# A two-layer graph network: edge product in the second sweep, node stage inside the first

## The chip, the cores and the metric

The kernel runs on one core of one Trainium2 chip. The time is the device time of one execution in microseconds (us). Before the change three runs gave 4691.19 us as their median (4682.67 to 4695.08).

## What is computed

12,500 nodes with 128 numbers each, and 200,000 edges whose targets `dst` are sorted and lie densest at low node numbers (target = 12500·u², u uniform). Two layers follow each other; here without the weights' small print:

```python
h = relu(layernorm(x))                                        # layer 0
neigh = segment_sum(h[src], dst)
x = x + relu(relu(((1 + eps) * h + neigh) @ W1 + b1) @ W2 + b2)
h = relu(layernorm(x))                                        # layer 1
hn = layernorm(h) * gamma + beta
t = gelu(concat([hn[src], edge_attr]) @ Wt + bt)              # per edge
attn = sum((t @ Wk + bk) * (hn[dst] @ Wq + bq)) * edge_weight / sqrt(128)
a = softmax of attn over the edges of one target
aggr = segment_sum(a * (t @ Wv + bv), dst)
out = x + h + gelu(aggr)
```

The concatenation is split: `hn @ Wt[:128] + bt` is made once per node ("source rows") and gathered per edge; `edge_attr @ Wt[128:]` is the edge product.

## The kernel before

Edges are worked in 98 chunks of 2048. A chunk is 8 blocks of 256 edges, or 16 columns of 128 edges; four columns make a quad, so a chunk has 4 quads. All of a chunk's targets of a block lie in a window of 40 nodes, and all of the chunk's in 264 nodes (SPAN), so sums are made by small one-hot products and added into `acc`, [128, nodes], at a position that registers hold. Each engine has its own written-out program; they meet through semaphores. Loops over chunks are unrolled by four (`over_chunks` for two stages, `over_stages` for four), so an engine takes one branch back every fourth chunk.

The program has seven parts, one after the other, with barriers of all engines and clearing of semaphores (`Stage.clear`) between them:

- `constants`, `node_norm` (layer norm of x, rows `h0`, first term of `acc`), `edge_tables` (start of each window).
- `gin_sweeps`, the first sweep. For each chunk GpSimd issues 16 indirect DMAs of 128 rows (`gather_chunk`, L506) from `h0`, after a one-element instruction (`hold`, L500). TensorE makes the edge product of the chunk from `edge_attr_cols` (L572, 16 products of 128x128), ScalarE copies it (L602) and writes it to HBM as `edge_products`; then TensorE sums the chunk's gathered rows (L583) and VectorE adds them to `acc` (L629). Four gather buffers `hs`.
- `node_mid`: 14 groups of 896 nodes go through W1, W2, two norms, Wt, Wq and Wk. It writes the residual rows, the source rows and `qk`, `ck`.
- A setup block: `acc` and `rows` are set to their first values by VectorE and GpSimd.
- `attention_sweeps`, the second sweep, in four stages. For chunk n: GpSimd gathers source rows into `t` (four buffers), VectorE adds the edge product, read back from HBM, in place (L1123), ScalarE applies gelu in place (L1079), TensorE turns each quad (L988) and ScalarE copies it out as `tT` (L1084), TensorE makes scores against the window's `qk` (L1003). One step later the maxima pass through TensorE (L1012, L1021, L1027) and VectorE (L1183 to L1216), ScalarE makes the exponentials (L1093); another step later TensorE sums `t` by them (L1040) and the totals (L1047); VectorE adds these (L1170 to L1177).
- `node_end`: 14 groups: Wv, division, gelu, output.

What holds a gather up: the chunk's index list has landed, the buffer is free (`sums_ready` of four chunks ago in the first sweep, `t_used` in the second). Both sweeps sit in a loop over windows that runs once for these inputs.

## Time and profile before

| | us |
|---|---|
| three runs, median | 4691.19 |
| the profiled execution, its own time | 4713.18 |
| its span | 4711.2 |
| first sweep's gathers, first to last | 139.3 to 2128.5 |
| from there to the second sweep's first gather | 314.4 |
| second sweep's gathers | 2442.9 to 4526.0 |
| from there to the end of the span | 185.2 |

The profile gives busy time by engine: PE is TensorE's products, PEld its weight loads, DVE is VectorE, ACT ScalarE, POOL GpSimd, SP the engine that issues most DMAs. Time in which an engine issues DMAs or handles registers and semaphores isn't counted as busy.
### The profile page before, as it was taken

How to read it: one execution, taken by the hardware profiler on the slowest of the kernel's cores; microseconds unless marked ns; L12 is line 12 of the kernel's file. 1: busy time of each engine (PE TensorE's matmuls, PEld its weight loads, DVE VectorE, ACT ScalarE, POOL GpSimd, SP SyncE). 2: the span in 40 equal slices, each digit the busy share in tenths (PEclk: the TensorE clock that was granted, in tenths of full speed). 3: DMA queues.
4: the chain of work that ended last, by engine and by line, in shares of the span. 5: the costliest groups of instructions: out<-in, count | busy, mean ns of one | idle time of the engine just before them, and what ended most of it. 6: DMA issues, size and time to landing. Idle time of an engine off the chain costs nothing. (4 is left out here: it accounts for less than half of the span.)

```text
span 4711.2 us, 72968 instructions
## 1 busy us (share of the span) xinstructions
PE 3054.1 (65%) x20056; PEld 2809.9 (60%) x20057; DVE 1865.5 (40%) x5996; ACT 1313.3 (28%) x2114; POOL 3162.9 (67%) x3343
## 2 busy tenths in 40 slices
PE   2466666556665666664746777676767777777774
PEld 1466566556665666663326767676666666766664
DVE  3111111111111111114545666666666666666643
ACT  4111111111111111113633343343333343434324
POOL 0677777777777777770037777777777777777730
PEclk9666666666666666667877787788888787888776
DMA  4455445555455545542334444444444444444423
GB/s 123 150 159 159 148 152 159 159 159 157 144 158 159 159 144 156 159 141 64 102 101 115 125 122 117 113 127 121 118 124 116 124 116 123 117 126 118 121 61 101
DMA packets 364892, 614.69 MB, mean 130 GB/s; under 512 B 109604, under 2 KB 237335, under 8 KB 339624
## 3 DMA queue, kind: packets, MB, share of 16 engines
q1 hardware_dynamic: 237284, 298.04, 22.2%
q0 software_dynamic: 100352, 205.72, 16.9%
q10 hardware_dynamic: 27076, 109.29, 5.6%
q14 instruction: 160, 1.31, 0.1%
q8 instruction: 20, 0.33, 0.0%
HBM read 477.54 MB, written 135.23 MB: 130 GB/s over the span
## 5 line engine op out<-in xcount | busy, mean ns | idle before, releaser
L506 POOL DMA_INDIRECT attention_t<-source_rows,attention_idx x1568 | 1587.9, 1013 | 463.4 <-issue 447.7
L506 POOL DMA_INDIRECT gin_hs<-h_rows,gin_idx x1568 | 1506.7, 961 | 463.1 <-issue 463.0
L583 PE MATMUL gin_sums<-gin_hot,gin_hs 128*128 128x40 f32 x3136 | 686.6, 413 | 763.7 <-DMA gin_hs<-h_rows,gin_idx 763.7
L583 PEld LDWEIGHTS gin_sums<-gin_hot,gin_hs 128*128 128x128 f32 x3136 | 672.5, 330 | 781.8 <-issue 725.0
L629 DVE TENSOR_TENSOR acc<-acc,gin_sums 128x40 f32 x784 | 154.5, 197 | 1760.7 <-PE gin_sums L583 1670.3
L602 ACT ACTIVATE gin_ews<-gin_ew_ps 128x512 f32<-128x512 f32 x392 | 234.1, 597 | 1768.3 <-PE gin_ew_ps L572 1768.0
L988 PE MATMUL attention_tT_ps<-ident,attention_t 128*128 128x128 f32 x1568 | 366.5, 378 | 385.4 <-ACT attention_t L1079 385.4
L572 PE MATMUL gin_ew_ps<-gin_wt_edge,gin_evT 128*128 128x128 f32 x3136 | 566.2, 363 | 7.6 <-DMA gin_evT<-in_edge_attr_cols 7.6
L572 PEld LDWEIGHTS gin_ew_ps<-gin_wt_edge,gin_evT 128*128 128x128 f32 x3136 | 554.1, 277 | 8.9 <-DMA gin_evT<-in_edge_attr_cols 8.8
L988 PEld LDWEIGHTS attention_tT_ps<-ident,attention_t 128*128 128x128 f32 x1568 | 266.9, 199 | 421.8 <-issue 367.1
L1003 PE MATMUL attention_sc_q<-attention_qw,attention_tT 128*128 x3136 | 515.6, 325 | 1.2
L1003 PEld LDWEIGHTS attention_sc_q<-attention_qw,attention_tT 128*128 128x128 f32 x3136 | 504.3, 245 | 8.3 <-issue 4.2
L1079 ACT ACTIVATE attention_t<-attention_t 128x512 f32<-128x512 f32 x392 | 243.0, 627 | 548.6 <-DVE attention_t L1123 548.6
L1084 ACT ACTIVATE attention_tT<-attention_tT_ps 128x512 f32<-128x512 f32 x392 | 234.1, 597 | 550.6 <-PE attention_tT_ps L988 550.4
L1040 PE MATMUL attention_sum_ps<-attention_e_hot,attention_t 128*128 128x96 f32 x3136 | 375.3, 278 | 0.0
L1040 PEld LDWEIGHTS attention_sum_ps<-attention_e_hot,attention_t 128*128 128x128 f32 x3136 | 359.3, 192 | 12.3 <-issue 0.2
L1123 DVE TENSOR_TENSOR attention_t<-attention_t,attention_ews 128x512 f32<-128x512 f32 x392 | 251.1, 690 | 223.2 <-DMA attention_t<-source_rows,attention_idx 163.3
L1021 PE MATMUL attention_row_bank<-ident,attention_bm 80*1 80x80 f32 x784 | 97.5, 287 | 192.6 <-DVE attention_bm L1183 192.3
L1200 DVE TENSOR_TENSOR attention_mnew<-attention_mnew,attention_row_bank 1x40 f32 x784 | 144.3, 184 | 188.0 <-issue 61.6
L1216 DVE TENSOR_TENSOR attention_below<-attention_masked,attention_row_bank 128x80 f32<-128x80 f32 x784 | 126.7, 231 | 201.6 <-PE attention_row_bank L1027 196.9
L922 POOL MEMSET rows<- 1x12928 f32 x1 | 10.9, 10863 | 279.6 <-POOLq L640 279.6
L1021 PEld LDWEIGHTS attention_row_bank<-ident,attention_bm 80*1 80x1 f32 x784 | 67.7, 101 | 213.2 <-DVE attention_bm L1183 198.2
(137 smaller groups left out, 2958.2 us busy)
## 6 DMA issues: line engine op xcount, KB each, us to landing
gin_evT<-in_edge_attr_cols SPq DMA_DIRECT2D x98, 1024.0 KB, 6.6
edge_products<-gin_ews ACTq DMA_DIRECT2D x98, 1024.0 KB
attention_ews<-edge_products SPq DMA_DIRECT2D x392, 256.0 KB
gin_hs<-h_rows,gin_idx POOLq DMA_INDIRECT x1568
attention_t<-source_rows,attention_idx POOLq DMA_INDIRECT x1568
attention_qw<-qk_cols SPq DMA_DIRECT2D x98, 160.0 KB
attention_cw<-qk_bias_cols SPq DMA_DIRECT2D x98, 132.0 KB
attention_fade<-fades SPq DMA_DIRECT2D x98, 132.0 KB
```

The source lines that it names most:

```text
L506: gp.indirect_dma_start(out=out[:, k, :], out_offset=None, in_=rows[:, :], compute_op=op, in_offset=bass.IndirectOffsetOnAxis(ap=idx[:, k: ...
L572: mm = pe.matmul(ew_ps[q % 2][:, k * P:(k + 1) * P], evT[f.j][:, at:at + P], wt[:, :], start=True, stop=True)
L583: mm = pe.matmul(sums[j][:, b * WIN:(b + 1) * WIN], hs[bk.k][:, k, :], hot[j][:, k, :], start=(k % SUB == 0), stop=(k % SUB == SUB - 1))
L602: act.activation(ews[f.j][:, 4 * q:4 * q + 4, :].rearrange("p k d -> p (k d)"), ew_ps[q % 2][:, :], ACT.Copy).then_inc(ew_sb, 1)
L629: v.tensor_tensor(g["acc"][:, bass.ds(at, WIN)], g["acc"][:, bass.ds(at, WIN)], sums[bk.j][:, b * WIN:(b + 1) * WIN], ALU.add).then_inc(ad ...
L988: mm = pe.transpose(tT_ps[q % 2][:, k * P:(k + 1) * P], t[f.k][:, 4 * q + k, :], g["ident"][:, :])
L1003: mm = pe.matmul(sc_ps[:, o:o + WIDE], tT[q % 2][:, (n % 4) * P:(n % 4 + 1) * P], qw[j][:, bass.ds(off, WIDE)], start=True, stop=True)
L1021: mm = pe.matmul(row_bank[0:1, k * 2 * WIN:(k + 1) * 2 * WIN], bm[:, k:k + 1], g["ident"][0:2 * WIN, 0:2 * WIN], start=True, stop=True)
L1040: mm = pe.matmul(sum_ps[:, bass.ds(off, WIDE)], t[bk.k][:, k, :], e_hot[j][:, k, :], start=False, stop=True, skip_group_check=True)
L1079: act.activation(x, x, ACT.Gelu).then_inc(s["t_sb"], 1)
L1084: act.activation(tT[q % 2][:, :], tT_ps[q % 2][:, :], ACT.Copy).then_inc(s["tT_sb"], 1)
L1123: v.tensor_tensor(x, x, ews[q][:, :, :], ALU.add).then_inc(s["summed"], 1)
```

## The change

Three things, and what they need.

**The edge product moves to the second sweep.** The first sweep no longer reads `edge_attr_cols` and writes no `edge_products`. In the second, TensorE turns the raw gathered rows of a quad into one PSUM bank `pre_ps` (4 turns) and adds the edge product there, one product with `w_edge` stationary and 512 columns moving, on top of them (`turn_rows`). ScalarE's gelu reads that bank and writes `tT`. TensorE turns `tT` back (`turn_gelu`, into `t_ps`) and ScalarE copies that over the raw rows in `t` (`copy_t`). VectorE's four additions per chunk are gone; SP loads the edge attributes in two halves of 512 KB per chunk instead of four pieces of 256 KB of `edge_products`.

**The node stage runs inside the first sweep.** Since targets are sorted, `acc` is final below the next chunk's lowest target. `edge_tables` computes for each chunk a position (`spots`), and every chunk's step takes 256 nodes from there through what `node_mid` did (`first_product` to `by_target`, `relu` to `norm2`, `residual` to `renorm`). 98 windows of 256 cover 12,544 nodes with overlap; a loop over six stages (`over_stages(..., 6, MID_PEEL)`) spreads a window over the steps after its chunk. If the positions don't reach the last nodes in one sweep, `span` is raised so that another follows; for these inputs they reach them.

**Loops and borders.** The loops over chunks get a prefetch hint for their branch and start at the head of a fetch block (`engine_loop`). `Stage.clear` (up to three barriers, each semaphore cleared alone) becomes `done` or `renew` (one barrier, ranges cleared). Window tables, the first values of `acc` and `rows`, and the loads of weights are issued outside blocks of their own, so that GpSimd goes from one sweep into the next without waiting for them; chunk 0's index list `idx0` is loaded at the start of the program. `rows` is set by ScalarE, the rest by VectorE.

```diff
-    def clear(self, gathers=False):
-        self.nc.all_engine_barrier()
-        if gathers:
-            self.nc.gpsimd.dma_reset()
-            self.nc.all_engine_barrier()
-        for s in self.sems:
-            self.nc.sync.sem_clear(s)
-        self.nc.all_engine_barrier()
+    def renew(self):
+        self.nc.gpsimd.dma_reset()
+        self.done()
...
 def gin_sweeps
-                    def step(f, bk):
-                        if f:
-                            for q in range(QUADS):
-                                edge_product(f, q)
+                    def step(f, bk, p1, p2, r4, a5):
+                        if p2:
+                            turn(p2)
+                        if p1:
+                            first_product(p1)
+                            second_product(p1)
+                        if p2:
+                            by_source(p2)
+                            by_target(p2)
                         if bk:
                             add_rows(bk)
...
+                    def first_product(m):
+                        at = spot(pe, u_reg, g, m.c)
+                        wait(pe, added, (m.c + 1) * BPC)
+                        wait(pe, s["u_sb"], m.c)
+                        pe.matmul(u_ps, W["W1"][:, :], g["acc"][:, bass.ds(at, MW)], start=True, stop=True).then_inc(s["u_ps"], 1)
...
 def attention_sweeps
+                    def turn_rows(f, q):
+                        c, h, j = f.c, f.h, f.j
+                        wait(pe, gathered[f.k][q], 64 * (f.g + 1))
+                        wait(pe, s["tT_sb"], QUADS * c + q)
+                        for k in range(4):
+                            pe.matmul(pre_ps[:, k * P:(k + 1) * P], t[f.k][:, 4 * q + k, :], g["ident"][:, :], is_transpose=True,
+                                      start=(k == 0), stop=False, skip_group_check=True)
+                        if q % 2 == 0:
+                            wait(pe, ev_in[q // 2], 16 * (c + 1))
+                        pe.matmul(pre_ps[:, :], w_edge[:, :], evT[q // 2][:, 512 * (q % 2):512 * (q % 2 + 1)],
+                                  start=False, stop=True, skip_group_check=True).then_inc(s["pre_ps"], 1)
...
                         if f:
                             load_offsets(pe, pe_regs[f.k], g, f.c)
-                            turn_gelu(f, 0)
+                            turn_rows(f, 0)
                         if mid:
                             turn_scores(mid)
                         if f:
-                            turn_gelu(f, 1)
+                            turn_rows(f, 1)
+                            turn_gelu(f, 0)
                             scores(f, 0)
                         if mid:
                             spread_maxima(mid)
                         if f:
+                            turn_rows(f, 2)
+                            turn_gelu(f, 1)
+                            scores(f, 1)
+                            turn_rows(f, 3)
                             turn_gelu(f, 2)
-                            scores(f, 1)
+                            scores(f, 2)
                             turn_gelu(f, 3)
-                            scores(f, 2)
                             scores(f, 3)
...
                     def gelu(f, q):
-                        wait(act, s["summed"], QUADS * f.c + q + 1)
-                        x = t[f.k][:, 4 * q:4 * q + 4, :]
-                        act.activation(x, x, ACT.Gelu).then_inc(s["t_sb"], 1)
+                        wait(act, s["pre_ps"], QUADS * f.c + q + 1)
+                        wait(act, s["t_ps"], QUADS * f.c + q - 1)
                         wait(act, s["sc_q"], QUADS * f.c + q - 1)
-                        act.activation(tT[q % 2][:, :], tT_ps[q % 2][:, :], ACT.Copy).then_inc(s["tT_sb"], 1)
+                        act.activation(tT[q % 2][:, :], pre_ps[:, :], ACT.Gelu).then_inc(s["tT_sb"], 1)
...
-                    def add_products(f):
-                        for q in range(QUADS):
-                            wait(v, ew_in[q], 16 * (f.c + 1))
-                            wait(v, gathered[f.k][q], 64 * (f.g + 1))
-                            x = t[f.k][:, 4 * q:4 * q + 4, :]
-                            v.tensor_tensor(x, x, ews[q][:, :, :], ALU.add).then_inc(s["summed"], 1)
```

How instructions stand on two engines now. TensorE at the head of a chunk in the second sweep, before (a register load, turns of the finished quad 0, of the last chunk's maxima, of quad 1, then scores):

```order
L483 TENSOR_LOAD offset
L70 ISA
L70 REGISTER_ALU
L988 MATMUL attention_tT_ps<-ident,attention_t 128x128 x4
L70 REGISTER_ALU
L1012 MATMUL attention_xm_bank<-ident,attention_xm 80x128 x4
L70 REGISTER_ALU
L988 MATMUL attention_tT_ps<-ident,attention_t 128x128 x4
L70 ISA
L493 ISA
L1003 MATMUL attention_sc_q<-attention_qw,attention_tT 128x96 x2
```

And after (L1057 turns raw rows, L1061 adds the edge product, L1069 turns back):

```order
L584 TENSOR_LOAD offset
L75 REGISTER_ALU
L1057 MATMUL attention_pre_ps<-ident,attention_t 128x128 x4
L75 ISA
L1061 MATMUL attention_pre_ps<-attention_evT,attention_w_edge 128x512
L1092 MATMUL attention_xm_bank<-ident,attention_xm 80x128 x4
L75 REGISTER_ALU
L1057 MATMUL attention_pre_ps<-ident,attention_t 128x128 x4
L1061 MATMUL attention_pre_ps<-attention_evT,attention_w_edge 128x512
L1069 MATMUL attention_t_ps<-ident,attention_tT 128x128 x4
L594 ISA
L1083 MATMUL attention_sc_q<-attention_qw,attention_tT 128x96 x2
```

Ahead of the first scores stand now three groups of four turns of the chunk's own rows instead of two, and two wide products.

GpSimd from the first sweep's end into the second, before:

```order
L537 REGISTER_ALU [waits barrier_Pool_Activation_PE_DVE_SP_gather]
L537 REGISTER_ALU
L537 COMPARE_AND_BRANCH
L920 UNCONDITIONAL_BRANCH [waits barrier_Pool_Activation_PE_DVE_SP_gather]
L922 MEMSET rows 1x12928
L925 MEMSET attention_e_hot 128x1536 [waits constants_ones_ready] x2
L927 MEMSET rows 1x6464 [waits constants_ones_ready]
L903 UNCONDITIONAL_BRANCH [waits constants_ones_ready]
L930 UNCONDITIONAL_BRANCH [waits barrier_Pool_Activation_PE_DVE_SP_gather]
L969 UNCONDITIONAL_BRANCH [waits barrier_Pool_Activation_PE_DVE_SP_gather]
L500 TENSOR_TENSOR spare<-ones 1x1 [waits attention_idx_in_0]
L506 DMA attention_t<-source_rows,attention_idx 128x128 x16
```

And after:

```order
L641 DMA gin_hs<-h_rows,gin_idx 128x128 x16
L699 UNCONDITIONAL_BRANCH
L698 REGISTER_ALU [waits barrier_Pool_Activation_PE_DVE_SP_gather]
L698 REGISTER_ALU
L698 COMPARE_AND_BRANCH
L994 UNCONDITIONAL_BRANCH
L1034 UNCONDITIONAL_BRANCH
L635 TENSOR_TENSOR spare<-ones 1x1
L641 DMA attention_t<-source_rows,idx 128x128 x16
```

One barrier is left between the two sweeps' gathers, no memset and no wait for an index list.

## Rows read from the trace of the kernel before

**Rows 1.** Three stretches: busy PE, PEld, DVE, ACT, POOL; clock, DMA, GB/s.

```profile
139.00:2128.00 1989.00, 1226.49 (x6240) 1208.24 (x6240) 230.44 (x872) 234.10 (x392) 1524.25 (x1666) 0.63 0.51 155
2128.00:2443.00 315.00, 179.10 (x750) 103.32 (x750) 152.58 (x577) 147.09 (x295) 19.84 (x7) 0.78 0.29 85
2443.00:4526.00 2083.00, 1517.35 (x12280) 1382.85 (x12281) 1358.52 (x4045) 813.36 (x1164) 1617.97 (x1665) 0.80 0.44 120
```

**Rows 2.** The page's costliest groups: busy us, mean ns | idle before, ended by.

```profile
L506 POOL DMA_INDIRECT attention_t<-source_rows,attention_idx x1568 | 1587.9, 1013 | 463.4 <-issue 447.7
L506 POOL DMA_INDIRECT gin_hs<-h_rows,gin_idx x1568 | 1506.7, 961 | 463.1 <-issue 463.0
...
L1123 DVE TENSOR_TENSOR attention_t<-attention_t,attention_ews 128x512 f32<-128x512 f32 x392 | 251.1, 690 | 223.2 <-DMA attention_t<-source_rows,attention_idx 163.3
```

**Rows 3.** Timeline, GpSimd: start us, duration; first and last gathers of both sweeps.

```profile
139.31 1.13 POOL L506 DMA_INDIRECT gin_hs<-h_rows,gin_idx  x1 [0.17 <-issue]
...
2127.50 0.95 POOL L506 DMA_INDIRECT gin_hs<-h_rows,gin_idx  x1 [0.30 <-issue]
...
2442.88 0.98 POOL L506 DMA_INDIRECT attention_t<-source_rows,attention_idx  x1 [0.15 <-issue]
...
4525.03 0.95 POOL L506 DMA_INDIRECT attention_t<-source_rows,attention_idx  x1 [0.31 <-issue]
```

**Rows 4.** Timeline between the edge tables and the first gather.

```profile
123.48 0.96 DVE L416 TENSOR_REDUCE span<-edge_wide 1x1 int32<-1x784 f32 x1
...
137.33 0.34 SPq L548 DMA_DIRECT2D gin_idx<-in_src_chunks  x1
```

**Rows 5.** Timeline from the first sweep's last sums to the second's tables.

```profile
2132.75 7.05 PE L583 MATMUL gin_sums<-gin_hot,gin_hs 128*128 128x40 f32 x32 [14.70 <-DMA gin_hs<-h_rows,gin_idx]
2139.94 2.49 DVE L629 TENSOR_TENSOR acc<-acc,gin_sums 128x40 f32 x8 [19.26 <-PE gin_sums L583]
...
2410.79 10.83 DVE L915 MEMSET acc<- 128x12928 f32 x1 [12.09 <-issue]
...
2434.37 0.61 DVE L440 TENSOR_SCALAR attention_t<-start 1x882 f32<-1x882 f32 x1 [5.85 <-PEq L196]
```

**Rows 6.** The node stage: timeline of two products of 448 columns; a group.

```profile
2397.34 1.67 PE L729 MATMUL node_mid_pa<-node_mid_m_hT,node_mid_w_Wq 128*128 128x448 f32 x4
```
```profile
L779 ACT ACTIVATE node_mid_m_u<-node_mid_pa,node_mid_c_b 128x896 f32<-128x896 f32 x14 | 14.0, 1004 | 57.6 <-PE node_mid_pa L729 57.6
```

**Rows 7.** Timeline, TensorE, one chunk of the second sweep, head to head.

```profile
3318.40 1.11 PE L988 MATMUL attention_tT_ps<-ident,attention_t 128*128 128x128 f32 x4 [5.81 <-ACT attention_t L1079]
...
3324.88 0.60 PE L988 MATMUL attention_tT_ps<-ident,attention_t 128*128 128x128 f32 x4
3325.32 2.06 PE L1003 MATMUL attention_sc_q<-attention_qw,attention_tT 128*128 x16
3327.31 0.71 PE L1027 MATMUL attention_row_bank<-attention_mnew,ones 1*128 1x264 f32 x2
...
3336.31 1.11 PE L988 MATMUL attention_tT_ps<-ident,attention_t 128*128 128x128 f32 x4 [2.94 <-ACT attention_t L1079]
```

**Rows 8.** The register loads of L483 on TensorE; two VectorE rows of that chunk.

```profile
L483 PEldq TENSOR_LOAD <-offset x98: 587/591/612, 2440.5 to 4520.6; - x98
```
```profile
3328.15 1.27 DVE L1216 TENSOR_TENSOR attention_below<-attention_masked,attention_row_bank 128x80 f32<-128x80 f32 x8 [1.06 <-PE attention_row_bank L1027]
...
3334.43 0.49 DVE L1161 TENSOR_TENSOR attention_xm<-attention_masked 128x320 f32<-128x320 f32 x1
```

**Rows 9.** Busy time and granted clock in two stretches of that chunk (columns as in Rows 1).

```profile
3318.40:3322.50 4.10, 4.10 (x20) 4.01 (x20) 3.94 (x8) 2.70 (x5) 3.19 (x4) 0.50 0.78 223
3322.60:3333.30 10.70, 10.59 (x110) 9.47 (x108) 7.01 (x30) 4.92 (x6) 8.15 (x9) 1.00 0.41 120
```

**Rows 10.** Timeline, the second sweep's last quad: VectorE's addition, TensorE's running maxima.

```profile
4530.13 0.69 DVE L1123 TENSOR_TENSOR attention_t<-attention_t,attention_ews 128x512 f32<-128x512 f32 x1 [5.63 <-DMA attention_t<-source_rows,attention_idx]
```
```profile
4541.90 0.71 PE L1027 MATMUL attention_row_bank<-attention_mnew,ones 1*128 1x264 f32 x2
```

783 lines of the change are left out of this document (421 added, 362 removed).

## The prediction, made before the changed kernel ran

> **What bounds the kernel now.** I read the busy time by stretch first, then the costliest groups, then the waits at the places where one stage hands over to the next. The two sweeps take 1989 and 2083 of 4711 us, the node stage with the setup 315 between them, and the rest is start and end [rows 1]. In both sweeps GpSimd is never kept waiting by another engine for long: of its idle time 463 and 448 us are gaps of 0.30 us between one gather and the next [rows 2, 3], which belong to issuing. 1568 gathers take 139.3 to 2128.5 us in the first sweep, 20.3 us per chunk of 16, and 2442.9 to 4526.0 in the second, 21.26 per chunk [rows 3]. So GpSimd's issuing of gathers is the bound of both sweeps, and everything else runs beside it. What this bound doesn't cover are four pieces: the start (139.3), the gap (314.4), the end (185.2), and whatever makes a gather longer.
>
> **The start.** The index list's load and wait (137.33 to 139.31) goes, and the window tables that ran ahead of it are now made beside gathers. From the span's reduction (ending at 124.4) to the first gather are 14.9 us [rows 3, 4]. Some 25 short VectorE instructions for the positions are added at about 0.2 us each (the shortest VectorE steps of the trace are that long), 5 us. I leave 3 us for the barrier and the branch: 14.9 becomes 8, so -7 (bounds -12 and +3).
>
> **The first sweep.** What goes (edge product, its copy, its write) was beside the gathers: 0. What comes is a node step of 256 columns per chunk. Its cost is nothing as long as its chain fits into 20.3 us, so I add the chain up, with TensorE at half clock (it was granted 0.63 here [rows 1]). TensorE sums the chunk's rows, 7.05, and VectorE adds them, 2.5 [rows 5]. Then W1 on 256 columns: two products of 448 take 1.67 at full clock [rows 6], so 256 columns take 0.45, at half 0.9, and 0.25 to drain; relu 0.4 (an estimate from 1.0 for 896 columns [rows 6]); W2 1.1; on VectorE bias, residual, statistics 1.6; deviation 0.3; then Wq's result is copied 0.4 and Wk and bk are applied 1.7, and TensorE is free for the next sums. Hand-overs add 1. Sum 7.05 + 2.5 + 1.15 + 0.4 + 1.1 + 1.6 + 0.3 + 0.4 + 1.7 + 1 = 17.2 us, 3 below the pace. Source products and the second norm lie beside the last of these. The gathers of the next chunks don't hang on it, for there are four buffers. SP's stores per chunk (three of 128 KB and one of 1 KB, a load of 128 KB) replace 2 MB. If the chain were longer than 20.4, each us would cost 98.
>
> More VectorE work lengthens gathers: their mean is 961 ns in the first sweep and 1013 in the second [rows 2], 81 us in all, for 1128 us more of VectorE's time [rows 1], 0.072 us each. The first sweep gains about 4.5 us of VectorE's time per chunk, but little of it is of the long kind: +20 us, bounds 0 and +45.
>
> **The gap.** 314.4 us go [rows 3]. In their place: the last gather lands 4.3 us after its end (2128.45 to 2132.75), its sums 7.05 and additions 2.5 [rows 5]; then the last window goes alone through its node step, in two steps of the pipeline, of which I count for the first 10 us (from W1 to the end of the second norm) and for the second 6 (turn to Wk), both from the terms above; 3 for the stores to land; 5 for the barrier, the reset of GpSimd's queue and the clearing (the old ones with three barriers took 5.85 [rows 5]). Sum 38. So -276 (bounds -283 and -262). Setting `acc` (10.8 us) and the tables stay, but GpSimd goes on gathering beside them: four buffers of chunks hide the 26 us by which TensorE starts later than the gathers.
>
> **The second sweep** is where it could go wrong, since TensorE gets 16 more turns and 4 wide products per chunk. I take one chunk at its shortest, head 3318.40 to head 3336.31, 17.91 us [rows 7]. Of it 2.94 is a wait at the end for ScalarE's gelu, and 4.10 us ran at the clock's level of 0.50, the rest at 1.00 [rows 9]. At the full level that is 17.91 - 2.94 - 2.05 = 12.9 us of work and small waits. Added: four turns take 0.44 at the full level (3324.88 to 3325.32) [rows 7], four times 1.8 us; a product of 512 columns 0.85 to 0.95 (from 1.67 for two of 448 [rows 6]), four times 3.4 to 3.8. That gives 18.1 to 18.5. New waits: each quad's rows go TensorE, ScalarE, TensorE through one bank; turns of maxima, scores and the other quad's products stand between, so that I find only 0.3 us ahead of the second quad and 0.3 to 0.5 ahead of the last turn back. Sum 19.2.
>
> Does the wait of 2.94 stay? It looks like a cost of TensorE's own (a register load stands there), but that load takes 0.59 us [rows 8] and runs while the last products do. The wait is the chain through VectorE: from the running maxima (3327.31) its steps end with `xm` at 3334.92 [rows 7, 8], then came an addition and a gelu. The change takes these two out: the new head waits only for gathered rows. What is late next is `xm` itself, 7.6 us after the running maxima, where TensorE needs 6.1 and the first quad's 1.3: 0.2 to 0.3 us. So TensorE's chunk is 19.4, beneath the gathers' pace of about 21. While it has idle time left, a fall of the clock costs 1.7 to 2 us, and what is then used up is that idle time; hence I count nothing.
>
> The gathers then set the pace. VectorE loses 251 us of additions [rows 2]: at 0.072 that is 18 us, and since these are long instructions with both operands in SBUF I take -30 (bounds 0 and -81). ScalarE's load stays the same, eight passes of 512 per chunk. SP's loads are again 1 MB per chunk, and their buffers come free early in TensorE's order.
>
> A rule of the Trainium skill speaks against this. The rows show that TensorE's level went from 0.50 to 1.00 4.1 us after the head, in a stretch that was for the most part turns [rows 9]. The page "TensorE: Matmul & The Clock Gate", section "Part 4: PE-mode transpose", says that turns don't count as busy for the clock. By the row they do; by the rule 32 turns per chunk would hold the level down, and the time would be that of the third rival.
>
> **The end.** Before, the last quad was added at 4530.13 and the running maxima followed at 4541.90 [rows 10]; the other quads' work waited behind that addition in VectorE's order. Now turn, product, two turns back and two groups of scores follow, 1.3 + 2.7 + 0.3: 4534.5. So -7.
>
> **Sum.** -7 + 20 - 276 - 30 - 7 - 2 (fewer barriers elsewhere) = -302. The profiled execution took 4713.2 and would take 4411. It was 22 us above the median of the three runs; from the median, 4389 us.
>
> **Rivals.**
> - *TensorE is the bound of the second sweep at the clock as it is now.* It was granted 0.80 on the mean [rows 1]. 18.3 / 0.80 + 1.1 = 24.0 us per chunk at worst; half-way between this and 19.4, 22.2, is what I hold likelier. For: its idle time drew down the level in almost every chunk. Against: the cause was the waits, which mostly go. 98 x (22.2 - 20.9) = +127: 4516. At 24.0 it would be +304, no change: 4693.
> - *The node step is the bound of the first sweep.* The chain would have to be 3.2 us longer than I count to matter; with 22 us per chunk 98 x 1.5 = +147: 4536. Against: its terms are at half clock already.
> - *Slower: the level of the clock stays at 0.50 through the turns.* From the head to the running maxima TensorE would do its 12 us of work at half speed, 24, and the chunk takes some 31 us: 98 x (31 - 20.9) = +990, 5380. It decides against the change from 24.0 us per chunk on, that is, from about 5 us of loss per chunk. Against it are the rows on the clock.
> - *A second run of a sweep,* if the positions didn't reach the last node. The targets grow by at most some 250 nodes per chunk and a window has 256, so it doesn't happen.
>
> **Numbers.** Forecast 0.72 (within 4335 to 4460), TensorE bound at 22 or so 0.10, at 24 or a little more 0.05, node step 0.06, clock held down 0.05, other 0.02. The range 4335 to 4545 leaves out the last few of these. A measurement of this kernel can tell about 0.3% from no change, 14 us: faster 0.91, same 0.02, slower 0.07.
>
> **What would show it.** In the profile after: first gather at about 132 us; 20.5 us per chunk in the first sweep, with VectorE's and TensorE's node steps beside it; 38 us between the sweeps' gathers; in the second sweep 20.9 us per chunk, GpSimd's idle time still ended by its own issuing, and TensorE waiting 1 to 2 us per chunk for gathered rows; clock near 1.0 there. The prediction is wrong if GpSimd waits for `t_used` (TensorE is the bound) or for `sums_ready` (the node step is), or if the gap is over 60 us.

## The result, and the profile after

The changed kernel took 4369.4 us (median of four runs, 4356.7 to 4372.5), the kernel before 4687.9 (four runs); the ratio is 0.9315, with a 95% interval of 0.9291 to 0.9338. The profiled execution took 4369.9 us with a span of 4368.1. The forecast was 4389, within 4335 to 4545.

The busy time by stretch: first sweep, gap, second sweep, end (columns: PE, PEld, DVE, ACT, POOL busy; TensorE's clock, DMA share, GB/s).

```profile
128.90:2124.80 1995.90, 1318.47 (x4842) 1004.68 (x4842) 588.69 (x2431) 402.61 (x1061) 1531.55 (x1665) 0.52 0.30 78
2124.80:2160.00 35.20, 18.75 (x62) 12.64 (x62) 5.91 (x27) 7.49 (x18) 0.18 (x1) 0.50 0.16 31
2160.00:4191.80 2031.80, 1802.58 (x14650) 1422.89 (x14651) 1142.75 (x3677) 803.43 (x1166) 1558.31 (x1665) 0.99 0.43 123
4191.80:4368.00 176.20, 94.92 (x644) 88.45 (x643) 65.20 (x215) 62.54 (x137) 0.00 (x0) 0.68 0.29 76
```

Against [rows 1], the stretch of 315 us has become 35, TensorE's clock in the second sweep went from 0.80 to 0.99, and in the first from 0.63 to 0.52. GpSimd's timeline has the ends of the stretches:

```profile
128.92 1.12 POOL L641 DMA_INDIRECT gin_hs<-h_rows,idx  x1 [0.64 <-issue]
...
2123.83 0.94 POOL L641 DMA_INDIRECT gin_hs<-h_rows,gin_idx  x1 [0.30 <-issue]
2159.31 0.18 POOL L635 TENSOR_TENSOR spare<-ones 1x1 f32<-1x1 f32 x1 [34.54 <-POOLq L233]
2160.01 0.97 POOL L641 DMA_INDIRECT attention_t<-source_rows,idx  x1 [0.51 <-issue]
...
2188.99 0.18 POOL L635 TENSOR_TENSOR spare<-ones 1x1 f32<-1x1 f32 x1 [9.04 <-DMA attention_idx<-in_src_chunks]
...
4190.66 1.13 POOL L641 DMA_INDIRECT attention_t<-source_rows,attention_idx  x1 [0.30 <-issue]
```

With [rows 3] this gives the account of the two profiled executions:

| | before, us | after, us | difference | forecast |
|---|---|---|---|---|
| start to first gather | 139.3 | 128.9 | -10.4 | -7 |
| first sweep's gathers | 1989.1 | 1995.9 | +6.7 | +20 |
| gap between the sweeps' gathers | 314.4 | 35.2 | -279.2 | -276 |
| second sweep's gathers | 2083.1 | 2031.8 | -51.3 | -30 |
| last gather to the end | 185.2 | 176.3 | -8.9 | -7 |
| outside of the span, barriers | 2.0 | 1.8 | -0.2 | -2 |
| sum | 4713.2 | 4369.9 | -343.3 | -302 |

The medians differ by 318.5 us and these two executions by 343.3, since the profiled one before took 25 us more than the median before. So the differences in the table are together some 25 us larger than those of a usual execution; in which rows this lies is not shown.

GpSimd is still the bound. Its two groups on the page (the counterpart of [rows 2]) have idle time that its own issuing ends, and the mean gather of the second sweep is 983 ns, where it was 1013:

```profile
L641 POOL DMA_INDIRECT attention_t<-source_rows,attention_idx x1552 | 1524.9, 983 | 458.2 <-issue 450.4
L641 POOL DMA_INDIRECT gin_hs<-h_rows,gin_idx x1552 | 1497.9, 965 | 458.1 <-issue 458.0
```

TensorE's waits in the second sweep, 2160 to 4192 (us in total, times, longest), and the three places of one chunk where it stands (the counterpart of [rows 7]; the turns are L1057, the head is at 3333.87):

```profile
PE attention_pre_ps L1057 <- ACT attention_tT L1165: 140.6, 96, 1.7
PE attention_pre_ps L1057 <- DMA attention_t<-source_rows,attention_idx: 34.0, 56, 2.7
...
PE attention_pre_ps L1057 <- issue: 16.7, 26, 0.9
```
```profile
3322.90 0.65 PE L1057 MATMUL attention_pre_ps<-ident,attention_t 128*128 128x128 f32 x4 [0.37 <-DMA attention_t<-source_rows,attention_idx]
...
3333.87 0.65 PE L1057 MATMUL attention_pre_ps<-ident,attention_t 128*128 128x128 f32 x4 [0.70 <-issue]
...
3337.49 0.65 PE L1057 MATMUL attention_pre_ps<-ident,attention_t 128*128 128x128 f32 x4 [1.66 <-ACT attention_tT L1165]
```

The wait of 2.9 at the head is gone; it is 0.1 as a rule and 0.7 at every fourth chunk. But TensorE waits only 34 us in the whole sweep for gathered rows, 0.35 per chunk: the bound is GpSimd by a hair.

In the first sweep the node step stands between the sums. TensorE waits for VectorE's additions (2.29) and, before the next sums, 3.40 for gathered rows:

```profile
303.18 1.21 PE L769 MATMUL gin_uy_bank<-acc,gin_w_W 128*128 x2 [2.29 <-DVE acc L908]
...
314.38 7.02 PE L761 MATMUL gin_sums<-gin_hot,gin_hs 128*128 128x40 f32 x32 [3.40 <-DMA gin_hs<-h_rows,gin_idx]
```

### The profile page after: what moved, and what is told of

Read it like the earlier page. It is cut to its first block and busy times, and to the rows that moved or that the text cites. A ratio compares the mean times of both kernels' runs of the same rounds, so it can differ in the third digit from the quotient of the medians.

```text
span 4368.1 us, 76943 instructions
## 1 busy us (share of the span) xinstructions
PE 3263.8 (75%) x20322; PEld 2550.8 (58%) x20323; DVE 1854.9 (42%) x6646; ACT 1332.0 (30%) x2507; POOL 3091.4 (71%) x3341
## 5 line engine op out<-in xcount | busy, mean ns | idle before, releaser
L1165 ACT ACTIVATE attention_tT<-attention_pre_ps 128x512 f32<-128x512 f32 x392 | 234.1, 597 | 626.7 <-PE attention_pre_ps L1061 625.7
L1057 PE MATMUL attention_pre_ps<-ident,attention_t 128*128 128x128 f32 x1568 | 257.2, 287 | 203.9 <-ACT attention_tT L1165 140.6
L1061 PE MATMUL attention_pre_ps<-attention_evT,attention_w_edge 128*128 128x512 f32 x784 | 404.9, 598 | 2.6 <-DMA attention_evT<-in_edge_attr_cols 2.6
L1083 PE MATMUL attention_sc_q<-attention_qw,attention_tT 128*128 x3136 | 405.7, 272 | 0.0
L1083 PEld LDWEIGHTS attention_sc_q<-attention_qw,attention_tT 128*128 128x128 f32 x3136 | 383.2, 193 | 0.0
L1121 PEld LDWEIGHTS attention_sum_ps<-attention_e_hot,attention_t 128*128 128x128 f32 x3136 | 360.7, 193 | 12.3 <-issue 0.2
L1057 PEld LDWEIGHTS attention_pre_ps<-ident,attention_t 128*128 128x128 f32 x1568 | 165.5, 141 | 269.8 <-ACT attention_tT L1165 163.0
L769 PE MATMUL gin_uy_bank<-acc,gin_w_W 128*128 x196 | 119.2, 711 | 228.2 <-DVE acc L908 228.2
L1069 PEld LDWEIGHTS attention_t_ps<-ident,attention_tT 128*128 128x128 f32 x1568 | 189.5, 142 | 165.6 <-issue 156.2
L1169 ACT ACTIVATE attention_t<-attention_t_ps 128x512 f32<-128x512 f32 x392 | 232.4, 593 | 80.9 <-PE attention_t_ps L1069 80.9
L1069 PE MATMUL attention_t_ps<-ident,attention_tT 128*128 128x128 f32 x1568 | 239.5, 276 | 0.0
```

What stands on the lines that cost most here:

```text
L769: pe.matmul(u_ps, W["W1"][:, :], g["acc"][:, bass.ds(at, MW)], start=True, stop=True).then_inc(s["u_ps"], 1)
L1057: pe.matmul(pre_ps[:, k * P:(k + 1) * P], t[f.k][:, 4 * q + k, :], g["ident"][:, :], is_transpose=True, start=(k == 0), stop=False, skip_g ...
L1061: pe.matmul(pre_ps[:, :], w_edge[:, :], evT[q // 2][:, 512 * (q % 2):512 * (q % 2 + 1)], start=False, stop=True, skip_group_check=True).th ...
L1069: mm = pe.transpose(t_ps[:, k * P:(k + 1) * P], tT[q % 2][:, k * P:(k + 1) * P], g["ident"][:, :])
L1083: mm = pe.matmul(sc_ps[:, o:o + WIDE], tT[q % 2][:, (n % 4) * P:(n % 4 + 1) * P], qw[j][:, bass.ds(off, WIDE)], start=True, stop=True)
L1121: mm = pe.matmul(sum_ps[:, bass.ds(off, WIDE)], t[bk.k][:, k, :], e_hot[j][:, k, :], start=False, stop=True, skip_group_check=True)
```

## The experiments

"Theory" is at first that of the prediction: GpSimd's gathers are the bound, and VectorE's work lengthens them. The spans of a sweep are from its first gather's start to its last one's end, as above. The kernel before was timed anew beside each group of runs (medians 4687.9, 4698.6 and 4689.5 us), so totals are compared by their ratios. Their intervals are 0.0023 to 0.0031 to either side, 11 to 15 us; what differs by less is read from the sweeps' spans in the profiled executions.

### The node stage back between the sweeps (node_apart)

```diff
+        node_mid(nc, a, g, res, arow, qk, ck)      # as in the kernel before
                     def step(f, bk, p1, p2, r4, a5):
-                        if p2:
-                            turn(p2)
-                        if p1:
-                            first_product(p1)
...
                         if bk:
                             add_rows(bk)
```

> Only the other half of the change: the node step is taken out of the first sweep and runs between the sweeps as the stage of the kernel before, while the edge product stays in the second sweep and the loops as changed. Theory (the gap is a plain sum of stages; the node step inside the sweep costs its gathers little): the gap between the sweeps' gathers goes from 35 back to about 300 us, the first sweep's gathers go from 1996 to 1990 us, the second sweep stays at 2032: 4369 + 265 - 6 = 4628, range 4610 to 4645. Rival (the node step inside costs the first sweep's gathers as much as VectorE's work does in the second, 20 us or more): the first sweep 1976 or less.

Measured: 4612.7 us, ratio 0.9829 (0.9805 to 0.9853). The gap is 275.7 us, of which GpSimd's own row has 275.04:

```profile
2408.08 0.18 POOL L636 TENSOR_TENSOR spare<-ones 1x1 f32<-1x1 f32 x1 [275.04 <-POOLq L234]
```

The total fell where I expected it, the parts did not: the gap came out at 276 where I had counted 300. So of the 279 us, 240 are the node stage's place. The other 39 are all the rest that changed at this border (`acc` and the tables made beside gathers, fewer barriers, the loads of weights), which no run takes apart. And the first sweep did not become shorter when the node step left it: 2002.5 us for 1995.9. Its gathers and the stretch from 140 to 2110 us show the same; in the kernel of this run:

```profile
140.00:2110.00 1970.00, 676.20 (x3072) 662.50 (x3072) 228.25 (x864) 0.00 (x0) 1513.16 (x1639) 0.50 0.20 52
```
```profile
L642 POOL DMA_INDIRECT gin_hs<-h_rows,gin_idx x1534 | 1487.8, 970 | 452.7 <-issue 452.7
```

VectorE is busy 228 us there, in the changed kernel 581, and yet a gather takes 970 ns here and 965 there. A price per us of VectorE's time, as the prediction had, can't be right.

### More work on TensorE in the first sweep (edge_in_first_too, node_dose)

```diff
                         if p2:
                             turn(p2)
+                        if f:
+                            edge_product(f, 0)
+                            edge_product(f, 1)
...
                             by_target(p2)
+                        if f:
+                            edge_product(f, 2)
+                            edge_product(f, 3)
```

> The changed kernel with the edge product made a second time in the first sweep, as the kernel before made it (1 MB loaded, four products per quad of 4 x 128 columns, a copy, 1 MB written, per chunk; nobody reads it, the output stays the reference's). It asks whether the node step could have moved in without the edge product moving out. Theory A (TensorE at the level of 0.50, where it is in that sweep): its chain of 17.5 us per chunk grows by 4 x 2.1 = 8.3, of which the wait of 2.3 for VectorE's additions takes in some; 23.5 per chunk, 4369 + 98 x 3.1 = 4670, range 4600 to 4800. Theory B (a TensorE with less idle time gets the full level in part, and the chain shrinks by as much as it grew): 4369 to 4400, granted clock in the first sweep 0.65 or more.

```diff
+                        for _ in range(8):
+                            pe.matmul(q_ps, W["Wq"][:, :], hT[:, :], start=True, stop=True)
                         pe.matmul(q_ps, W["Wq"][:, :], hT[:, :], start=True, stop=True).then_inc(s["q_ps"], 1)
```

> The changed kernel with eight more products of 256 columns (the one of Wq again) in each node step, on the chain between the source rows and the query: 8 x 0.53 at the full level is 4.2 us per chunk... at the level of 0.50 it is 8 x 0.85 = 6.8. TensorE waits 3.0 us per chunk for gathered rows in the first sweep. Theory A (the level stays at 0.50): 98 x (6.8 - 3.0) = +370, 4369 becomes 4740, down to 4500 if one such product takes 0.55. Theory B (the level rises as TensorE's idle time goes, so the chain fits again): 4365 to 4400, and the clock in the first sweep above 0.60.

Measured: 4355.6 us (ratio 0.9283, 0.9252 to 0.9314) with the edge product, 4368.2 (0.9312, 0.9288 to 0.9335) with the eight products: theory B in both. The stretch from 140 to 2110 us in the changed kernel, with the edge product, and with the dose:

```profile
140.00:2110.00 1970.00, 1305.29 (x4805) 996.73 (x4806) 580.99 (x2404) 399.32 (x1052) 1511.48 (x1646) 0.52 0.30 78
```
```profile
140.00:2110.00 1970.00, 1406.10 (x7978) 1225.93 (x7976) 585.25 (x2429) 611.83 (x1450) 1508.46 (x1655) 0.77 0.57 182
```
```profile
140.00:2110.00 1970.00, 1493.34 (x6345) 1200.20 (x6344) 582.48 (x2409) 398.66 (x1052) 1509.93 (x1651) 0.69 0.29 78
```

The granted clock went from 0.52 to 0.77 and 0.69, and TensorE's busy time grew by only 101 us with the edge product, where it ran two thirds more instructions and DMA moved 182 GB/s for 78. So work that I had counted at 7 to 8 us per chunk at the lower level went in at no cost. That settles two things. The chain of the node step, 17.5 us by its rows, was not 3 us from being the bound; it had a cushion in the clock. And the edge product didn't have to leave the first sweep to make room for the node step: with both in it the sweep took 1983 us. The 12 us by which that is shorter than the changed kernel's are all in the gathers' durations (summed over 0.945 us each: 19 for 32), which the last group of runs explains. The edge product was made in both sweeps here; a kernel with the node step in the first sweep and the second sweep as before was not run.

### TensorE's margin in the second sweep (no_edge, edge_plus1, turns_for_edge)

```diff
-                        pe.matmul(pre_ps[:, :], w_edge[:, :], evT[q // 2][...],
-                                  start=False, stop=True, skip_group_check=True).then_inc(s["pre_ps"], 1)
+                        mm.then_inc(s["pre_ps"], 1)      # mm: the last of the four turns
```

> The changed kernel without the wide edge product in the second sweep; the columns of edge attributes are still loaded, the turns into PSUM stay. So the edge term is left out of the attention's rows. TensorE has 4.1 us less to do per chunk. Theory (GpSimd's gathers bound the second sweep): 4369 becomes 4355 to 4375; TensorE's new idle time shows as waits for gathered rows of about 4 us per chunk, and the granted clock falls from 0.99 below 0.90. Rival (TensorE sets the pace in part, through the buffers of rows it frees): 4369 becomes 4330 to 4350, the sweep's chunk 20.4 us or less.

```diff
+                        if q == 3:
+                            pe.matmul(pre_ps[:, :], w_edge[:, :], evT[q // 2][...], start=True, stop=True)
                         for k in range(4):
                             pe.matmul(pre_ps[:, k * P:(k + 1) * P], t[f.k][:, 4 * q + k, :], ... is_transpose=True, ...)
```

> The changed kernel with one more product of 512 columns per chunk in the second sweep (made into the bank ahead of the last quad's turns, which write over it; the output stays the reference's): 0.85 us more per chunk on TensorE at the full level. TensorE's waits for gathered rows are 34 us in the whole sweep, 0.35 per chunk. Theory (TensorE is that close behind the gathers): it becomes the bound, 98 x (0.85 - 0.35) = +50 us, 4369 becomes 4400 to 4440, and GpSimd waits for freed buffers. Rival (the waits on ScalarE's gelu, 1.5 us per chunk, take the product in): 4369 to 4380.

```diff
+                        for k in range(4):
+                            pe.matmul(pre_ps[:, k * P:(k + 1) * P], evT[q // 2][...], g["ident"][:, :], is_transpose=True, ...)
...
-                        pe.matmul(pre_ps[:, :], w_edge[:, :], evT[q // 2][...], ...)
```

> The changed kernel with four turns of 128x128 of the edge attributes in the place of each product of 512 columns: the same number of columns through TensorE, but nearly half of its time in the second sweep is now turns (48 per chunk in place of 32). The edge term is left out of the attention's rows. Theory (turns count for the clock like products): granted clock 0.95 or more in the second sweep, 4369 stays within 4355 to 4385. Rival (turns don't count): the level falls to 0.50 in part of each chunk, TensorE needs several us more per chunk, and each us is 98: 4500 or more.

| | us | ratio to the kernel before | second sweep's gathers, us | per chunk |
|---|---|---|---|---|
| changed kernel | 4369.4 | 0.9315 (0.9291-0.9338) | 2031.8 | 20.73 |
| no_edge | 4353.9 | 0.9258 (0.9235-0.9281) | 2017.9 | 20.59 |
| edge_plus1 | 4401.8 | 0.9360 (0.9337-0.9383) | 2062.4 | 21.04 |
| turns_for_edge | 4370.7 | 0.9297 (0.9275-0.9319) | 2034.2 | 20.76 |

The stretch from 2200 to 4180 us, in the same order:

```profile
2200.00:4180.00 1980.00, 1774.44 (x14480) 1403.17 (x14479) 1114.03 (x3636) 783.77 (x1151) 1525.37 (x1631) 1.00 0.43 124
```
```profile
2200.00:4180.00 1980.00, 1570.01 (x13805) 1398.14 (x13804) 1121.51 (x3656) 795.63 (x1156) 1521.89 (x1642) 0.93 0.43 124
```
```profile
2200.00:4180.00 1980.00, 1808.56 (x14405) 1406.80 (x14403) 1092.67 (x3569) 769.16 (x1130) 1532.08 (x1606) 1.00 0.43 122
```
```profile
2200.00:4180.00 1980.00, 1645.34 (x15231) 1479.63 (x15231) 1113.67 (x3628) 783.70 (x1149) 1525.92 (x1629) 0.98 0.43 124
```

Without the product the pace stays GpSimd's: TensorE waits 205.8 us for gathered rows in place of 34.0, and the clock falls to 0.93 (I had expected below 0.90, and 4 us of waits per chunk; part of the time went into the lower clock and into waits for VectorE). The total is 1 us under the range of the theory, and the chunk of 20.59 us over the 20.4 of the rival. The sweep is 14 us shorter, and that is all in the gathers' own durations (summed over 0.945 us each: 44 us for 58), which has its explanation below.

With one product of 0.85 us more, TensorE's waits for gathered rows are gone altogether, its waits for the gelu are what they were (140.4 us for 140.6), and the pace is its own: three of four chunks take it 20.8 to 20.9 us (3300.10 to 3320.93 is one), the fourth, with the loop's end, 21.5. It falls behind until the buffers are used up: its first turn of a chunk stands 9.5 us behind the end of the chunk's fourth gather at chunk 6, 13.2 at chunk 18 and 13.1 to 13.9 from there on; in the changed kernel it is 6.9 to 7.9 throughout. The sweep is 30.6 us longer, 0.31 per chunk, so the margin was 0.85 - 0.31 = 0.54 us per chunk, an estimate. GpSimd shows little of that as waits: the instruction that holds it at a chunk's head took 46.8 us in all for 36.3 (both sweeps), and its gathers became 20 us longer, since more of them begin within VectorE's long instructions (89 for 43 within the one-hot, 92 for 55 within the first scalar_tensor_tensor); the last group of runs has what that costs.

In the last run, 738 of the 1645 us that TensorE was busy are the three groups of 128x128 turns, 45%, and the clock is 0.98:

```profile
L1059 PE MATMUL attention_pre_ps<-ident,attention_evT 128*128 128x128 f32 x1536 | 255.0, 289 | 304.1 <-DMA attention_t<-source_rows,attention_idx 155.4 <-ACT attention_tT L1167 116.6 <-issue 32.0
L1071 PE MATMUL attention_t_ps<-ident,attention_tT 128*128 128x128 f32 x1537 | 245.6, 285 | 0.0
L1062 PE MATMUL attention_pre_ps<-ident,attention_t 128*128 128x128 f32 x1536 | 237.3, 278 | 0.0
```

In these runs turns counted for the clock like products. The products alone are 907 us of the 1980, and yet the clock was 0.98; in the first sweep of edge_in_first_too 1406 us of 1970, nearly all products, were granted 0.77. The rule of the Trainium skill's page "TensorE: Matmul & The Clock Gate" (section "Part 4: PE-mode transpose"), by which they don't, does not hold for these float32 turns; the page's own durations are of bf16. Four turns take 0.44 us, half of what a product of 512 columns takes, so this kernel also had less to do; it is the clock that answers the question, not the time.

### The loops as they were (plain_loops)

```diff
-    return eng.bass.Fori(start, end, engines=[eng.engine], hint_back_edge=True, head_slot={eng.engine: 0})
+    return eng.Fori(start, end)
```

> The changed kernel with the loops written as before (no loop head at the head of an instruction block, no hint at the back edge). In the kernel before VectorE stood 2.6 us at every fourth chunk; now the longest stop at that place is 1.0. Theory A (TensorE is 0.4 to 0.5 us per chunk behind the gathers in the second sweep, and four chunks' slack is 1.6 to 2.0): the longer stop of VectorE and TensorE just uses it up, +0 to +40, 4370 to 4410. Theory B (it doesn't matter, GpSimd alone sets the time and its own loop stops are hidden in its queue): within 10 us of 4369.

Measured: 4362.4 us, ratio 0.9296 (0.9273 to 0.9319); sweeps of 1993.8 and 2027.1 us. Theory B: the form of the loops is worth nothing in time here, though VectorE stands 3.14 us at its loop's head (3334.96) where it is 0.70 in the changed kernel.

### What lengthens a gather (dve_adds, stt_adds, stt_forms, stt_forms_idx, iota_psum_idx)

```diff
                             raise_maxima(mid)
+                            for q in range(QUADS):
+                                wait(v, s["extra"], QUADS * mid.c + q)
+                                some = g["dst"][:, 0:256, :].rearrange("p b s -> p (b s)")
+                                v.tensor_tensor(some, some, some, ALU.max).then_inc(s["extra"], 1)
                             below_maxima(mid)
```

> The changed kernel, and in the second sweep four VectorE operations of 128x512 per chunk, source and destination in SBUF, as long as the addition that the change took out. They stand where VectorE waits 4.6 us per chunk for TensorE's running maxima, and nobody waits for them. The output stays the reference's. Theory (VectorE's work lengthens the gathers): the second sweep's gathers, 982 ns on the mean, go back towards the 1013 ns of the kernel before, the sweep becomes 40 to 55 us longer, 4369 becomes 4410 to 4425. Rival (the gathers became shorter since TensorE's or ScalarE's part changed): at most 10 us longer, 4369 to 4380, gathers stay at 982 ns.

Measured: 4418.5 us, ratio 0.9401 (0.9378 to 0.9424); the second sweep 2076.0 us, 44 longer, all of it in the gathers' durations (over 0.945 us each: 102 us for 58, of which 47 stand at the added instructions). The added work and the gathers:

```profile
L1311 DVE TENSOR_TENSOR dst<-dst 128x512 f32<-128x512 f32 x392 | 269.5, 687 | 10.0
```
```profile
L641 POOL DMA_INDIRECT attention_t<-source_rows,attention_idx x1552 | 1568.5, 1011 | 458.3 <-issue 434.4 <-PE attention_sum_ps L1121 14.9 <-DMA attention_idx<-in_src_chunks 8.8
```

So the shorter second sweep does come from the addition that VectorE no longer makes. But which property of VectorE's work is it? I went through all gathers of the traces by what VectorE did at the moment at which each began. In the changed kernel's first sweep 68 gathers began within a one-hot of 128x640, at least 0.035 us after its start and 0.05 before its end. They took 1.361 us on the mean, with 0.54 us of the one-hot left; a gather took 0.82 us plus what was left (correlation 1.00). The 1256 that began with VectorE idle, or within that distance of an instruction's start or end, took 0.947. Instructions that began after the gather had begun cost it nothing, and neither did reductions, memsets, or operations with one source in PSUM, however long. Two places of the changed kernel, a one-hot and a reduction, each with the gather that began within it:

```profile
201.00 0.82 DVE L568 TENSOR_TENSOR gin_hot<-iota,rel 128x640 f32<-128x640 f32 x1
```
```profile
201.18 1.46 POOL L641 DMA_INDIRECT gin_hs<-h_rows,gin_idx  x1 [0.30 <-issue]
```
```profile
2202.86 0.82 DVE L1228 TENSOR_REDUCE attention_attn<-attention_biased 128x16 f32<-128x640 f32 x1
```
```profile
2203.10 0.94 POOL L641 DMA_INDIRECT attention_t<-source_rows,attention_idx  x1 [0.30 <-issue]
```

The start of the instruction matters. Three gathers of that sweep and 35 of the second began 0.01 to 0.03 us after a VectorE operation of 128x640 with both sources in SBUF. They took the usual 0.94 to 0.95 us, and it was VectorE's operation that took longer, 0.86 to 0.89 us for 0.82. With the three in, the correlation over the first sweep's one-hots is 0.70. One such pair:

```profile
2241.74 0.88 DVE L1235 SCALAR_TENSOR_TENSOR attention_masked<-attention_miss,attention_attn 128x640 f32<-128x640 f32 x1
```
```profile
2241.76 0.94 POOL L641 DMA_INDIRECT attention_t<-source_rows,attention_idx  x1 [0.30 <-issue]
```

In the second sweep, 52 of the 58 us over 0.945 stand at three VectorE instructions of 128x640: 24.8 and 14.7 at the two scalar_tensor_tensor of the scores (L1225, L1235) and 12.3 at the one-hot.

Three runs asked about the form of the instruction, one about the place of its sources.

```diff
-                                v.tensor_tensor(some, some, some, ALU.max).then_inc(s["extra"], 1)
+                                v.scalar_tensor_tensor(out=some, in0=some, scalar=0.0, in1=some, op0=ALU.add, op1=ALU.max)...
```

> The run dve_adds again (four VectorE operations of 128x512 per chunk of the second sweep, both sources in SBUF), with each written as a scalar_tensor_tensor, (a + 0) max a, in the place of a tensor_tensor. dve_adds had made that sweep 44 us longer than the changed kernel's (2076 for 2032), the gathers 1010 ns for 982. Theory A (what lengthens a gather is the form tensor_tensor with both sources in SBUF; the rows of the two scalar_tensor_tensor of 128x640 showed next to no lengthening, 0.03 to 0.10 us per us beside a gather): the sweep stays at 2030 to 2045, 4365 to 4385. Theory B (any VectorE operation of that length with both sources in SBUF does it): 2065 to 2080, 4410 as dve_adds.

```diff
-    return v.tensor_tensor(out[:, :, :], g["iota"][:, :]..., rel..., op)      # and eight more of the two sweeps
+    return v.scalar_tensor_tensor(out=out[:, :, :], in0=g["iota"][:, :]..., scalar=0.0, in1=rel..., op0=ALU.add, op1=op)
```

> The changed kernel with every VectorE tensor_tensor of the two sweeps that has both sources in SBUF (the one-hots of 128x640, xm, the fades, the running maxima, the residual) written as a scalar_tensor_tensor with + 0; the output stays the reference's. Theory A (that form is what lengthens the gathers): gathers from 965 and 982 ns towards 950, the first sweep 25 us shorter (1996 to 1970), the second shorter until TensorE is the bound at some 20.2 us per chunk (2032 to 1985-2005): 4369 becomes 4295 to 4325. Theory B (the form doesn't matter): 4360 to 4375. In between, if the reduction of 128x640 is among the causes (0.54 us per us beside a gather in the changed kernel, 0.16 in dve_adds): 20 to 35 us of the second sweep's excess stay.

> The run stt_forms, and the second sweep's second index list loaded ahead of the window tables. In the changed kernel GpSimd waits 9.0 us for that list (the one stop of the sweep over 1 us). Theory A (the stop was a plain loss): 9 us less than stt_forms. Theory B (TensorE, which starts 23 us after the gathers, is then late to free the first buffers, and GpSimd waits there instead): same as stt_forms within 3 us in the sweep's span.

```diff
+        iota = st.ps("iota_bank")[:, 0:WIN]                  # and sum_ps[:, 512 - WIN:512] in the second sweep
+        nc.vector.tensor_copy(iota, g["iota"][:, :]).then_inc(spot_ready, 1)
-    return v.tensor_tensor(out[:, :, :], g["iota"][:, :].unsqueeze(1)..., rel..., op)
+    return v.tensor_tensor(out[:, :, :], iota.unsqueeze(1)..., rel..., op)
                         if f.at == 0:
+                            sp.dma_start(idx[1][:, :], src[1:2]...).then_inc(idx_in[1], 16)
                             sp.wait_ge(w["tables"], 7)
```

> The changed kernel with two edits; the output stays the reference's. One: the row 0..39 that both one-hots of 128x640 compare with (out<-iota,rel) lies in PSUM, so that these operations have one source in SBUF and one in PSUM. Two: the second sweep's second index list is loaded ahead of the window tables. Theory A, read from the traces of the earlier runs: a gather is lengthened only where a VectorE operation with both sources in SBUF is in progress as it begins, by as much as is left of it; with one source in PSUM, a reduction or a memset it never is. In the changed kernel 28 of the 32 us by which the first sweep's gathers are over 0.945 each stand at that one-hot, and 12 of 58 in the second. So the first sweep becomes 24 to 30 us shorter (1996 to 1966-1972), the second 5 to 20 by this and 9 by the list: 4369 becomes 4310 to 4335. Theory B (it is the length or the work of VectorE's operation, not where its sources lie): first sweep 1990 or more, 4355 to 4365. For the list: GpSimd's stop of 9.0 us goes; if TensorE is then late to free buffers, the stop comes back as a wait for them three chunks later.

These four ran on chips on which the kernel before took 6452 and 6462 us, with engines standing for up to 17 us with nothing that the profile shows them to wait for. Their totals (6241.7, 6246.3, 6253.0 and 6280.5 us, ratios of 0.968 to 0.971 with intervals of some 0.011) tell nothing of these edits. What a single gather takes beside a single instruction doesn't hang on those stops, and it answers the question. The one-hot as scalar_tensor_tensor, then the one-hot with a source in PSUM, each with the gather that began 0.2 us later:

```profile
492.42 0.83 DVE L566 SCALAR_TENSOR_TENSOR gin_hot<-iota,rel 128x640 f32<-128x640 f32 x1
```
```profile
492.64 1.42 POOL L646 DMA_INDIRECT gin_hs<-h_rows,gin_idx  x1 [0.30 <-issue]
```
```profile
492.44 0.83 DVE L568 TENSOR_TENSOR gin_hot<-gin_iota_bank,rel 128x640 f32<-128x640 f32 x1
```
```profile
492.62 0.94 POOL L641 DMA_INDIRECT gin_hs<-h_rows,gin_idx  x1 [0.31 <-issue]
```

By all the gathers of the first sweep that began within a one-hot, with the same distances as above: 1.206 us on the mean (54 of them, 0.38 us of the one-hot left) as tensor_tensor, in stt_adds; 1.209 (47, 0.37 left) as scalar_tensor_tensor, in stt_forms; 0.955 (51, 0.37 left) with one source in PSUM, in iota_psum_idx. The sum over 0.945 us of that sweep's gathers was 19.1, 13.5 and 2.8 us. In stt_adds 35 gathers began well within one of the added scalar_tensor_tensor of 128x512, and each took 0.82 us plus what was left, within 0.01. So my theory A of the runs on the form is wrong, the form doesn't matter. It rested on the rows of the changed kernel's own scalar_tensor_tensor, read as nearly free, and at L1235 30 of the 77 gathers that began within it did so in its first 0.03 us.

What matters for these instructions is that both sources are in SBUF. It isn't the only case: while the window tables are made, gathers that began within a VectorE operation of 1x882 with one source, a tensor_scalar or a copy that casts, followed the same sum (in the changed kernel 1.10 us with 0.29 left and 1.02 with 0.19 left; all 24 such gathers of the ten traces of runs on undisturbed chips did). They are too few to show in the time.

The Trainium skill's page "SBUF — State Buffer" (section "SBUF: two separate sides") has a VectorE operation with two SBUF inputs and a GpSimd operation that reads SBUF exclude one another for a whole instruction; the gather's list of indices lies in SBUF. The trace agrees where VectorE came first. Where the gather came first it doesn't: one-hots that began more than 0.1 us into a gather took their 0.82 to 0.83 us as ever, so VectorE didn't wait for the gather's 0.945.

Two things stay open. That a one-hot with a source in PSUM would shorten the changed kernel by the 28 us that its first sweep loses at the one-hots is an estimate from these rows, and not measured on an undisturbed chip. And with the index list loaded early the second chunk's gathers followed at once, but the third chunk then waited for its own list, 14.9 us in iota_psum_idx and 15.2 in stt_forms_idx, on those chips; whether the 9.0 us can be had is not shown. No version was shown to be faster than the changed kernel beyond the measurement.

## Why the prediction was right, step by step

- **The bound** was read rightly: GpSimd's issuing in both sweeps, before and after.
- **The gap** was forecast at 38 us and is 35.2. node_apart puts 240 of its 279 us to the node stage's place and 39 to the rest of the changes at that border.
- **The start and the end** were forecast at -7 each and came out at -10.4 and -8.9, from the same steps. At the start, 6.5 us are left between the span's reduction and the first gather for the 8 forecast: 4.2 for the positions (5) and 2.3 for barrier and branch (3). The reduction itself ends 2.0 us earlier, which is the separate term of -2 for barriers elsewhere. At the end, the running maxima follow the last gather's end by 7.8 us for 8.5 forecast and 15.9 before.
- **The first sweep** was forecast at +20 and is +6.7. The chain of the node step was counted at 17.2 us and takes 17.5 by its rows, so that it fits was right. The step that failed is the price, "0.072 us each" of VectorE's time. What costs is an operation with both sources in SBUF, and only where a gather begins within one. The node step has little of that kind, and the one-hots were there before: of 32 us over 0.945 per gather, 28.3 stand at the one-hots, where it was 20.9 of 25 before, since gathers now happen to begin in them more often. In the other runs in which VectorE does the same work in that sweep, on undisturbed chips, that sum is between 19 and 35 us, so the sign of the +6.7 is where the gathers fell and no cost of the node step.
- **The second sweep** was forecast at -30 and is -51.3. The direction was right by the same reasoning, and dve_adds puts the lost length back, +44. The size was off because I priced 251 us of additions by the mean of all VectorE's work. The gathers' durations fell by 47.6 us. A term that the prediction had not at all is the one-element instruction at the chunks' heads, 30.4 us in that sweep before and 18.3 now, -12.1. On the other side stands a stop of 9.0 us for the second index list, which the prediction didn't see: SP's loads stand behind its wait for the window tables, and that queue I had not followed to its first entries.
- **TensorE's chunk** was forecast at 19.4 us and takes 20.0 at its shortest, so that it waits 0.35 us per chunk for gathered rows and not 1 to 2. The work was right (18.1 to 18.5 forecast, 18.4 to 18.6 found, at the full level). The failed step is "only 0.3 us ahead of the second quad": TensorE has little to do between the first quad's product and the second's turns into the same bank, and waits 1.66 for the gelu between them. The margin to the gathers was therefore about 0.54 us per chunk and not 1.5, as edge_plus1 shows. With one product of 512 columns more per chunk the first rival's case begins.
- **That the head's wait goes** was right: 2.94 became 0.1, 0.7 at every fourth chunk. It was VectorE's chain, not TensorE's register load.
- **The rivals.** The node step as the bound of the first sweep was further off than its 0.06 says, since a busier TensorE got the full level for more of the time; the prediction had counted the chain at half clock and called that the safe side, and it is. TensorE as the bound of the second sweep was nearer than its 0.10 says. Its price has a slip: half-way between 24.0 and 19.4 is 21.7 and not 22.2, so +78 and 4467 in place of +127 and 4516; the forecast doesn't hang on it. The clock held down by turns did not happen: 0.99 with 32 turns per chunk, 0.98 with 48.
- **The sum.** Every stretch came out shorter than forecast, 41 us together in the profiled executions; by the medians the gain is 318 us for 302, since the profiled execution before lay 25 us above its median. The number was met because the large term, the gap, was right. The two sweeps' terms were off by 13 and 21 us in the same direction, above all by the one wrong price.

## What to carry to other kernels

Where one engine's issuing bounds a stretch, moving a stage beside it is worth that stage's whole time, and the sum of such moves can be made by stretches, as long as each moved chain fits into the pace. The margin of the next engine has to be added up with its waits at shared banks, not with its work alone; here it was about half a microsecond in twenty. Before pricing contention by busy time, sort the slowed instructions by what the other engine was doing as each began: here that turned a vague mean into a sum that holds gather by gather.

## What the runs showed of the hardware

- An indirect gather on GpSimd (128 rows of 512 bytes) took 0.945 us, or, where it began at least 0.05 us after the start of a VectorE operation with both sources in SBUF, 0.82 us plus what was left of that (1.361 us on the mean for 68 gathers with 0.54 left). The form (tensor_tensor, scalar_tensor_tensor) didn't matter; one source in PSUM (0.955 us), a reduction or a memset (0.94) cost it nothing. One-source operations of 1x882 in SBUF followed the sum too, in 24 gathers.
- Where the gather began 0.01 to 0.03 us after VectorE's operation, the gather lost nothing and VectorE 0.04 to 0.07 us (0.86 to 0.89 for 0.82). Where the one-hot began later within a gather, neither lost.
- TensorE with more to do was granted more clock: 0.50 with 676 us of busy time in 1970, 0.52 with 1305 (the changed kernel), 0.69 and 0.77 with the added products. The added work, 7 to 8 us per chunk if counted at the lower level, did not lengthen the sweep (1983 and 1988 us for 1996).
- Float32 turns of 128x128 counted for the clock as products do: 0.98 with 45% of the busy time in turns.
